# Six of sixteen injection products on GpSimd in one quarter of each Mamba step, and a regrouped opening

## The chip, the cores and the metric

The kernel runs on one core of a Trainium2 chip. The metric is the device time of one execution in microseconds (us). An execution uses five in-order engines: TensorE (PE, matrix products and transposes), VectorE (DVE), ScalarE (ACT), GpSimd (POOL) and SyncE (SP, here the queue from which DMAs are issued). Each engine runs its own list of instructions in order; semaphores are the only ties between them. An instruction that waits for a semaphore holds up all that stands behind it on its engine.

## What is computed

The model adds four sub-layers to a residual of 4096 tokens by 256 features: two Mamba layers (one call), a slot feed-forward network, windowed attention, and the feed-forward network again. The change is in the Mamba part alone, of which this is the core:

```python
def mamba(x, in_w, cw, cb, xp_w, dtp_w, dtp_b, A_log, Dp, out_w):
    ...
    xc = jax.nn.silu(xc)
    dbl = jnp.einsum('ble,re->blr', xc, xp_w)
    dt, Bm, Cm = jnp.split(dbl, [DT_RANK, DT_RANK + D_STATE], axis=-1)
    dt = jax.nn.softplus(jnp.einsum('blr,er->ble', dt, dtp_w) + dtp_b)
    A = -jnp.exp(A_log)
    dA = jnp.exp(dt[..., None] * A)
    dBu = (dt * xc)[..., None] * Bm[:, :, None, :]
    ...
    def step(h, inp):
        dA_t, dBu_t, C_t = inp
        h = dA_t * h + dBu_t
        y = jnp.einsum('ben,bn->be', h, C_t)
        return (h, y)
    ...
    y = ys.transpose(1, 0, 2) + xc * Dp
    y = y * jax.nn.silu(z)
    return jnp.einsum('ble,de->bld', y, out_w)
```

There are 512 inner channels e and 16 states n. `dBu` is what this text calls the injection.

## The kernel before

**Steps, units, quarters.** Each of two layers takes its 4096 tokens in 8 chunks of 512, so Mamba is 16 steps (`ALL`), written `s`. A step has 64 units `k` (`UNITS`): a unit is 4 states by 32 channels on the 128 partitions and 512 tokens along the row. Sixteen units make a quarter (`EG`), and a quarter holds four of the sixteen states for all channels. Four units make a quad. While step s scans, the projections, convolution, softplus and transposes of step p = s + 1 are woven in at fixed units, given by the tables of numbers at the top of the file (`D_...` for VectorE, `A_...` for ScalarE, `G_...` for GpSimd, `P_...` for TensorE).

**A unit.** ScalarE makes the decay, an exponential of 128x512 (`decay`, L541), at most 4 units ahead of the scan (`DEC`). TensorE transposes four 128x128 blocks of products into PSUM (`inject`, L771), at most 2 units ahead. VectorE runs the scan (L415). ScalarE copies the last column of four scanned units at a time (`keep`, L549), eight units after the quad's first in its own list; the copy of quad q stands at unit 4q + 8. GpSimd multiplies the scanned state by C (`output`, L640), in place, and waits at each quad's first unit for that copy (`carry`). TensorE then sums the states (L784).

**The products.** A quarter f = 4s + k//16 is injected from 16 products of 128x512, number j for token block j//4 and state j%4: `u_tok` (dt times x, tokens on partitions) times one column of `B_tok`. They are made one quarter ahead, into two buffers in turn (the names `k_r` and `u_B`). ScalarE makes 13 of them (L563), one at each unit after that unit's decay, and GpSimd three, numbers 3, 7 and 11 (`ON_POOL`), after its outputs of the units 0, 4 and 7 of the quarter (`G_PROD`, L629). At the first unit of a quarter `inject` waits for all sixteen, by two counts, `prod_a` and `prod_p`.

**Around the third quarter.** At unit 42 ScalarE loads the silu table, makes four silus of 128x512 (L512) and one of 128x2048 (L515) and loads the exponential table back; at unit 46 it does the same for softplus (L530, L533). From unit 47 on TensorE transposes the conv output and dt of the next step to tokens, one block after the other (`tok_x` L751, `tok_dt` L760), and VectorE copies the first (L380) and multiplies it by the second (L385) into `u_tok`.

**The opening.** Step s = -1 has no scans: it is the preparation of step 0 alone, and the 16 products of quarter 0 are its last work. On VectorE and TensorE the same blocks alternate one by one over two PSUM banks, each waiting for the one before to be read.

Of the kernel before, what the change touches and what calls it, by code (L numbers as in the profile page):

```python
# [12 lines left out]
P = 128  # L13
# [14 lines left out]
TB = T // P  # L28
# [18 lines left out]
PP = len(ON_POOL)  # L47
PA = NG * TB - PP
FIRST_A = [min(j for j in range(SG * tb, SG * tb + SG) if j not in ON_POOL) for tb in range(TB)]
LAST_V = 3  # L50
EARLY = 3
# [31 lines left out]
G_PROD = (0, 4, 7)  # L83
G_RSTD = 5
# [48 lines left out]
def mamba(nc, x, r, weights, consts, kept_r):  # L133
# [7 lines left out]
    with ExitStack() as ctx:  # L141
# [49 lines left out]
                 "b scan carry hc hc_v ysum prod_a prod_p gated o_mm res").split()  # L191
# [10 lines left out]
        conv_bank = lambda p, ct: PA_ + ct % 2 if p else CT + ct  # L202
        kc = lambda p, base, i, n=1: K[:, p // STEPS, base + i:base + i + n]
# [4 lines left out]
        with nc.Block() as block:  # L208
# [107 lines left out]
            def _(dve):  # L316
# [51 lines left out]
                def tok_B(p):  # L368
                    at(dve, "bt_mm", p + 1)
                    at(dve, "prod_a", PA * NG * (p - 1))  # L370
                    at(dve, "prod_p", PP * NG * (p - 1))
# [3 lines left out]
                def tok_x(p, tb):  # L375
                    at(dve, "xcT_mm", TB * p + tb + 1)
                    if p:
                        at(dve, "prod_a", PA * (NG * p - 1) + AFTER_A[tb])
                        at(dve, "prod_p", PP * (NG * p - 1) + AFTER_P[tb])
                    dve.tensor_copy(uT[:, tb], PS[:, PB_]).then_inc(S["xcT"], 1)  # L380

                def tok_u(p, tb):
                    at(dve, "dtT_mm", TB * p + tb + 1)
                    dve.wait_ge(S["xcT"], TB * p + tb + 1)
                    dve.tensor_tensor(uT[:, tb], PS[:, PA_], uT[:, tb], ALU.mult).then_inc(S["uT"], 1)  # L385
# [42 lines left out]
                for s in steps:  # L428
# [3 lines left out]
                    for k in range(UNITS):  # L432
# [29 lines left out]
                        if k == D_B:  # L462
                            tok_B(p)
                        for n in range(len(D_XT)):
                            if k == D_XT[n]:
                                tok_x(p, n)
                        for n in range(len(D_U)):
                            if k == D_U[n]:
# [3 lines left out]
            def _(act):  # L472
# [49 lines left out]
                def projected(p):  # L522
# [3 lines left out]
                    act.activation(dbl[:], PS[0:XW, PA_], ACT.Copy).then_inc(S["dbl"], 1)  # L526
# [40 lines left out]
                for s in steps:  # L567
                    p = s + 1
                    for k in range(UNITS):
# [5 lines left out]
                        if 0 <= f < ALL * NG and j not in ON_POOL:  # L575
# [4 lines left out]
                        if k == A_HALO and p < ALL:  # L580
                            halo(p)
                        if s < ALL and k == A_SILU:
                            silus(s)
                        if p >= ALL:
# [14 lines left out]
            def _(pool):  # L599
# [42 lines left out]
                for s in steps:  # L642
                    p = s + 1
                    for k in range(UNITS):
# [3 lines left out]
                        for n in range(PP):  # L648
# [1434 lines left out]
```

## Time and profile before

| | us |
|---|---|
| median of 3 executions | 2333.46 |
| lowest and highest | 2328.74, 2335.32 |
| the profiled execution | 2333.48 |
| its span | 2331.7 |
| TensorE, VectorE, ScalarE, GpSimd busy | 2067.5, 1880.3, 1795.9, 1654.9 |

The span is the stretch between the first and the last record. The Mamba part runs until about 1755 us of it. Its steps repeat: VectorE's first scan of a step stands at 62.78 us in step 0, and two equal stretches of 105.35 us that follow hold the same work. Busy shares are means over parts of the program with different limits, so single stretches are read below. "Idle before" in a row is what the engine waited just before it, with what ended the wait.

### The profile page before, as it was taken

What the parts mean: (1) busy time and instruction counts of PE and PEld (TensorE: products, weight loads), DVE (VectorE), ACT (ScalarE), POOL (GpSimd) and SP (SyncE); (2) the same over time, 40 slices, a digit from 0 to 9 for tenths busy, and PEclk for the clock granted to TensorE, in tenths of its full rate; (3) what the DMA queues carried; (4) which work ended last, traced back from release to release, by engine and by line L of the source; (5) the groups of instructions that cost most, each with busy time, mean ns of one, the idle gap of its engine ahead of it and who ended that gap; (6) DMA issues with size and microseconds to landing.
All of it is one profiled execution on the core that took longest, in us unless ns stands there. A gap on an engine that the chain in (4) does not pass through costs nothing. (4 is left out here: it accounts for less than half of the span.)

```text
span 2331.7 us, 40782 instructions
## 1 busy us (share of the span) xinstructions
PE 2067.5 (89%) x14787; PEld 1241.9 (53%) x14787; DVE 1880.3 (81%) x2584; ACT 1795.9 (77%) x3062; POOL 1654.9 (71%) x1448
## 2 busy tenths in 40 slices
PE   5989898998989898989989898989874879999987
PEld 2445455454545455554545454554533557777765
DVE  6788889898988889898988888888988656666655
ACT  3988998989898988989888989989864434455453
POOL 2789889898989889898989898898995253223110
PEclk9999999999999999999999999999996889999998
DMA  7340505142341515142331405041415000000012
GB/s 243 72 114 23 128 13 124 47 100 67 70 108 29 123 54 128 38 117 56 82 96 41 114 23 128 19 118 40 107 55 179 1 10 20 11 15 16 11 40 73
DMA packets 112237, 166.45 MB, mean 71 GB/s; under 512 B 13219, under 2 KB 58531, under 8 KB 111653
## 3 DMA queue, kind: packets, MB, share of 16 engines
q1 hardware_dynamic: 112036, 163.86, 26.8%
q8 instruction: 117, 1.92, 0.4%
q14 instruction: 84, 0.68, 0.1%
HBM read 125.53 MB, written 34.08 MB: 68 GB/s over the span
## 5 line engine op out<-in xcount | busy, mean ns | idle before, releaser
L640 POOL TENSOR_TENSOR h<-h,C_rep 128x512 f32<-128x512 f32 x1021 | 1270.5, 1277 | 196.3 <-ACT h_carry L549 196.3
L415 DVE TENSOR_TENSOR_SCAN h<-decay,h_carry,psum 128x512 f32<-128x512 f32 x768 | 955.7, 1270 | 126.5 <-PE psum L771 93.8
L541 ACT ACTIVATE decay<-dt_rep,A 128x512 f32<-128x512 f32 x1024 | 729.4, 713 | 96.6 <-DVE h L415 93.3
L771 PE MATMUL psum<-ident,u_B 128*128 128x128 f32 x2048 | 322.0, 282 | 125.1 <-DVE h L415 98.2
L771 PEld LDWEIGHTS psum<-ident,u_B 128*128 128x128 f32 x2048 | 235.2, 141 | 310.4 <-DVE h L415 215.2
L771 PEld LDWEIGHTS psum<-ident,k_r 128*128 128x128 f32 x2048 | 243.3, 142 | 248.8 <-issue 124.7
L415 DVE TENSOR_TENSOR_SCAN h<-decay,zero,psum 128x512 f32<-128x512 f32 x256 | 318.8, 1271 | 50.2 <-PE psum L771 34.7
L771 PE MATMUL psum<-ident,k_r 128*128 128x128 f32 x2048 | 309.9, 279 | 14.2 <-DVE h L415 9.0
L563 ACT ACTIVATE u_B<-u_tok,B_tok 128x512 f32<-128x512 f32 x416 | 295.1, 709 | 35.3 <-PE psum L771 35.3
L563 ACT ACTIVATE k_r<-u_tok,B_tok 128x512 f32<-128x512 f32 x416 | 294.4, 710 | 28.9 <-DVE u_tok L385 17.7
L784 PE MATMUL psum<-h,state_sum 128*32 128x512 f32 x2048 | 279.8, 619 | 3.6 <-POOL h L640 3.4
L694 PE MATMUL psum<-x_dt_gated,tap_diag 128*128 128x512 f32 x384 | 189.3, 597 | 0.0
L1773 DVE TENSOR_REDUCE a_row_max<-a_psum 128x4 f32<-128x512 f32 x128 | 87.6, 685 | 82.4 <-PE a_psum L1919 82.4
L1835 ACT ACTIVATE a_probs_T<-a_psum 128x512 f32<-128x512 f32 x128 | 69.6, 595 | 97.8 <-PE a_psum L1929 97.8
L673 PE MATMUL psum<-h_feat,w_x 128*128 128x512 f32 x256 | 135.0, 613 | 1.0 <-ACT h_feat L491 1.0
L673 PE MATMUL psum<-h_feat,w_z 128*128 128x512 f32 x256 | 131.2, 605 | 0.0
L799 PE MATMUL psum<-w_out,x_dt_gated 128*128 128x256 f32 x480 | 122.5, 383 | 0.0
L1839 ACT ACTIVATE a_probs<-a_probs 128x512 f32<-128x512 f32 x128 | 80.4, 629 | 50.1 <-DVE a_probs L1778 50.1
L629 POOL TENSOR_TENSOR k_r<-u_tok,B_tok 128x512 f32<-128x512 f32 x96 | 99.8, 1040 | 19.1 <-DVE u_tok L385 19.1
L629 POOL TENSOR_TENSOR u_B<-u_tok,B_tok 128x512 f32<-128x512 f32 x96 | 100.0, 1042 | 0.0
L1651 POOL TENSOR_TENSOR a_rstd<-a_vareps,a_minushalf 128x4 f32<-128x4 f32 x7 | 7.2, 1023 | 129.9 <-DVE a_vareps L1724 129.9
L799 PEld LDWEIGHTS psum<-w_out,x_dt_gated 128*128 128x128 f32 x480 | 84.2, 190 | 26.6 <-issue 19.7
(238 smaller groups left out, 2877.2 us busy)
## 6 DMA issues: line engine op xcount, KB each, us to landing
dt_rep<-dt_rows SPq DMA_DIRECT2D x256, 256.0 KB, 5.5
C_rep<-C_rows SPq DMA_DIRECT2D x256, 64.0 KB, 2.0
dt_rows<-x_dt_gated SPq DMA_DIRECT2D x32, 512.0 KB, 4.9
residual<-mamba_residual SPq DMA_DIRECT2D x16, 512.0 KB, 4.0
mamba_residual<-residual SPq DMA_DIRECT2D x16, 512.0 KB, 2.9
x_tok<-mamba_residual SPq DMA_DIRECT2D x15, 512.0 KB, 4.4
f_gru_weights<-in_slot_gru_dram SPq DMA_DIRECT2D x2, 2176.0 KB
u_B<-in_x_dram SPq DMA_DIRECT2D x8, 512.0 KB, 9.1
```

Of the source, the lines that this page charges most:

```text
L415: dve.tensor_tensor_scan(h[:, slot(u)], dec[:, u % DEC], PS[:, u % 2], first, ALU.mult, ALU.add)\
L541: act.activation(dec[:, u % DEC], dtr[:, k % EG], ACT.Exp, scale=A[:, s // STEPS, k:k + 1]).then_inc(S["decay"], 1)
L563: act.activation(pr[f % 2][:, tb, :, EW * n:EW * (n + 1)], uT[:, tb].rearrange("p (g e) -> p g e", e=EW), ACT.Copy, scale=BT[:, p % 2, tb, ...
L629: pool.tensor_tensor(pr[f % 2][:, tb, :, EW * n:EW * (n + 1)], uT[:, tb].rearrange("p (g e) -> p g e", e=EW), BT[:, p % 2, tb, SG * ng + n ...
L640: pool.tensor_tensor(h[:, slot(u)], h[:, slot(u)], crep[:, k // EG], ALU.mult).then_inc(S["hc"], 1)
L673: return pe.matmul(PS[:, bank], w[:, kt, ct * P:(ct + 1) * P], hT[:, kt], start=(kt == 0), stop=(kt == KT - 1))
L694: ins = pe.matmul(PS[:, conv_bank(p, ct)], TAPS[:, ct, j - 1], xs[:, ct, DC - 1 - j:DC - 1 - j + T], start=(j == 1), stop=(j == DC - 1))
L771: ins = pe.transpose(PS[:, u % 2, tb * P:(tb + 1) * P], pr[f % 2][:, tb, eg], ident[:])
L784: ins = pe.matmul(PS[EW * q:EW * (q + 1), YB + j % CT], sely[:], h[:, slot(q0 + q)], start=False, stop=(j >= QUADS - CT))
L799: ins = pe.matmul(PS[:, PA_ + i // 2, i % 2 * D:(i % 2 + 1) * D], g[:, ct, i * P:(i + 1) * P], WO[:, ct], start=(ct == 0), stop=(ct == CT ...
L1773: dve.tensor_reduce(mx[:, n % 2], PS[:, n % 2].rearrange("p (h t) -> p h t", h=4), AX, ALU.max)\
L1839: act.activation(pr[:, n % 4], pr[:, n % 4], ACT.Exp, scale=SCALE).then_inc(S["exp"], 1)
```

## The change

Three things are edited.

First, `LATE_POOL`: of the quarter that is formed during a step's third quarter (f % 4 == 3), GpSimd makes six products, numbers 3, 7, 9, 11, 13 and 15, after its outputs of the units 0, 4, 7, 9, 11 and 13 of that quarter (`G_LATE`), and ScalarE ten. The other three quarters keep three and thirteen. The counts that are waited for are now computed by `by_act` and `by_pool`. (`AFTER_P` and `AFTER_A` are written for `LATE_POOL` and a few lines on again for `ON_POOL`; the second holds.)

Second, quarter 0 of step 0: VectorE makes four of its products (`ON_DVE`, `first_product`, counted by `prod_v`), GpSimd three, ScalarE nine.

Third, the rest of the opening (p == 0): each silu waits for its own conv tile instead of for all four, the 12-column copy `halo` comes behind the silus, the x projection writes another PSUM bank, and the transposes of all four token blocks come in one go, conv output first and dt after, into eight different banks. VectorE reads them as four copies and four multiplies.

```diff
+LATE_POOL = (3, 7, 9, 11, 13, 15)
+on_pool = lambda f: LATE_POOL if f % NG == NG - 1 else ON_POOL
...
+def by_pool(f):
+
+    return sum(len(on_pool(e)) for e in range(f))
+
+
+def by_act(f):
+
+    return f * NG * TB - by_pool(f) - (PV if f > 0 else 0)
...
+ON_DVE = (2, 6, 10, 14)
+PV = len(ON_DVE)
...
+G_LATE = (0, 4, 7, 9, 11, 13)
...
+        xp_bank = lambda p: PA_ if p else CT
+        xt_bank = lambda p, tb: PB_ if p else YB + tb
+        dtt_bank = lambda p, tb: PA_ if p else (0, 1, PA_, PB_)[tb]
...
+                def first_product(j):
+
+                    tb, n = j // SG, j % SG
+                    at(dve, "uT", tb + 1)
+                    at(dve, "bt", 1)
+                    dve.tensor_scalar(pr[0][:, tb, :, EW * n:EW * (n + 1)], uT[:, tb].rearrange("p (g e) -> p g e", e=EW),
+                                      BT[:, 0, tb, n:n + 1], None, ALU.mult).then_inc(S["prod_v"], 1)
...
-                        at(act, "conv", CT * (s + 2))
                         for ct in range(CT):
+                            at(act, "conv", CT * (s + 1) + ct + 1)
...
-                        if 0 <= f < ALL * NG and j not in ON_POOL:
+                        if 0 <= f < ALL * NG and j not in on_pool(f) and (f or j not in ON_DVE):
                             product(f, j)
...
-                        for n in range(PP):
-                            if 0 <= f < ALL * NG and k % EG == G_PROD[n]:
-                                product(f, ON_POOL[n])
+                        for j, at_k in zip(on_pool(f), G_LATE if f % NG == NG - 1 else G_PROD):
+                            if 0 <= f < ALL * NG and k % EG == at_k:
+                                product(f, j)
...
                     if eg == 0:
-                        at(pe, "prod_a", PA * (f + 1))
-                        at(pe, "prod_p", PP * (f + 1))
+                        at(pe, "prod_a", by_act(f + 1))
+                        if f == 0:
+                            at(pe, "prod_v", PV)
+                        at(pe, "prod_p", by_pool(f + 1))
```

GpSimd in the third quarter of a step (units 36 to 48; L640 is an output of one unit, L629 a product), before:

```order
L640 TENSOR_TENSOR h<-h,C_rep 128x512 [waits m_carry]
L629 TENSOR_TENSOR u_B<-u_tok,B_tok 128x16x32 [waits m_b,m_bt,m_uT]
L640 TENSOR_TENSOR h<-h,C_rep 128x512 x3
L629 TENSOR_TENSOR u_B<-u_tok,B_tok 128x16x32 [waits m_b,m_bt,m_uT]
L640 TENSOR_TENSOR h<-h,C_rep 128x512 [waits m_carry]
L640 TENSOR_TENSOR h<-h,C_rep 128x512 x3
L640 TENSOR_TENSOR h<-h,C_rep 128x512 [waits m_carry]
L640 TENSOR_TENSOR h<-h,C_rep 128x512 x3
L640 TENSOR_TENSOR h<-h,C_rep 128x512 [waits m_C_loaded3,m_carry]
```

The same place now (L677 is the output, L666 the product):

```order
L677 TENSOR_TENSOR h<-h,C_rep 128x512 [waits m_carry]
L666 TENSOR_TENSOR u_B<-u_tok,B_tok 128x16x32 [waits m_b,m_bt,m_uT]
L677 TENSOR_TENSOR h<-h,C_rep 128x512 x3
L666 TENSOR_TENSOR u_B<-u_tok,B_tok 128x16x32 [waits m_b,m_bt,m_uT]
L677 TENSOR_TENSOR h<-h,C_rep 128x512 [waits m_carry]
L677 TENSOR_TENSOR h<-h,C_rep 128x512
L666 TENSOR_TENSOR u_B<-u_tok,B_tok 128x16x32 [waits m_b,m_bt,m_uT]
L677 TENSOR_TENSOR h<-h,C_rep 128x512 x2
L666 TENSOR_TENSOR u_B<-u_tok,B_tok 128x16x32 [waits m_b,m_bt,m_uT]
L677 TENSOR_TENSOR h<-h,C_rep 128x512 [waits m_carry]
L677 TENSOR_TENSOR h<-h,C_rep 128x512
L666 TENSOR_TENSOR u_B<-u_tok,B_tok 128x16x32 [waits m_b,m_bt,m_uT]
```

The last product moved from behind the output of unit 39 to behind that of unit 45, and two waits for `carry` (units 40 and 44) now stand ahead of it.

VectorE in the opening, from the copy of B to the first scans (L380 and L385 make `u_tok`, L415 is a scan), before:

```order
L372 COPY B_tok<-psum 128x64 [waits m_bt_mm]
L365 TENSOR_SCALAR x_dt_gated<-psum,small 128x512 [waits m_halo,m_dt_mm]
L365 TENSOR_SCALAR x_dt_gated<-psum,small 128x512 [waits m_dt_mm]
L380 COPY u_tok<-psum 128x512 [waits m_xcT_mm]
L385 TENSOR_TENSOR u_tok<-psum,u_tok 128x512 [waits m_xcT,m_dtT_mm]
...
L415 SCALAR_TENSOR_TENSOR h<-decay,zero,psum 128x512 [waits m_b,m_decay] x7
```

And now (L400 and L405 make `u_tok`, L412 is a product, L443 a scan):

```order
L392 COPY B_tok<-psum 128x64 [waits m_bt_mm]
L385 TENSOR_SCALAR x_dt_gated<-psum,small 128x512 [waits m_halo,m_dt_mm]
L385 TENSOR_SCALAR x_dt_gated<-psum,small 128x512 [waits m_dt_mm]
L400 COPY u_tok<-psum 128x512 [waits m_xcT_mm] x4
L405 TENSOR_TENSOR u_tok<-psum,u_tok 128x512 [waits m_xcT,m_dtT_mm] x4
L412 TENSOR_SCALAR k_r<-u_tok,B_tok 128x16x32 [waits m_bt,m_uT] x4
L443 SCALAR_TENSOR_TENSOR h<-decay,zero,psum 128x512 [waits m_b,m_decay] x7
```

Four alternating pairs became four copies, four multiplies and four products.

## Rows read from the trace of the kernel before

**Rows 1.** The page: busy us (share of span), instructions.

```profile
PE 2067.5 (89%) x14787; PEld 1241.9 (53%) x14787; DVE 1880.3 (81%) x2584; ACT 1795.9 (77%) x3062; POOL 1654.9 (71%) x1448
```

**Rows 2.** Windows: us; busy PE, PEld, DVE, ACT, POOL (instructions); clock; DMA; GB/s.

```profile
375.40:480.75 105.35, 96.59 (x542) 53.85 (x540) 92.22 (x94) 94.72 (x161) 92.79 (x81) 1.00 0.32 79
...
356.00:379.00 23.00, 16.79 (x121) 9.99 (x121) 22.59 (x24) 20.22 (x37) 22.88 (x20) 1.00 0.72 162
```

**Rows 3.** Timeline, GpSimd, step 2, units 36 to 48: start, us, instructions, idle before.

```profile
346.17 1.27 POOL L640 TENSOR_TENSOR h<-h,C_rep 128x512 f32<-128x512 f32 x1 [7.07 <-ACT h_carry L549]
347.40 1.03 POOL L629 TENSOR_TENSOR u_B<-u_tok,B_tok 128x512 f32<-128x512 f32 x1
348.40 3.74 POOL L640 TENSOR_TENSOR h<-h,C_rep 128x512 f32<-128x512 f32 x3
352.10 1.04 POOL L629 TENSOR_TENSOR u_B<-u_tok,B_tok 128x512 f32<-128x512 f32 x1
356.12 11.15 POOL L640 TENSOR_TENSOR h<-h,C_rep 128x512 f32<-128x512 f32 x9 [2.98 <-ACT h_carry L549]
```

**Rows 4.** Timeline, TensorE, step 2: transposes of unit 47, then of unit 48.

```profile
353.84 0.60 PE L760 MATMUL psum<-ident,x_dt_gated 128*128 128x128 f32 x4
356.00 0.66 PE L771 MATMUL psum<-ident,u_B 128*128 128x128 f32 x4 [1.55 <-ACT u_B L563]
```

**Rows 5.** Timeline, ScalarE, step 2: decay 47, last product, two carry copies.

```profile
354.61 0.72 ACT L541 ACTIVATE decay<-dt_rep,A 128x512 f32<-128x512 f32 x1
355.24 0.71 ACT L563 ACTIVATE u_B<-u_tok,B_tok 128x512 f32<-128x512 f32 x1
355.85 0.19 ACT L549 ACTIVATE h_carry<-h 128x4 f32<-128x4 f32 x1
...
360.24 0.20 ACT L549 ACTIVATE h_carry<-h 128x4 f32<-128x4 f32 x1
```

**Rows 6.** Timeline, VectorE, step 2: scan 47, copy, scan 48, end of the step.

```profile
355.45 1.27 DVE L415 TENSOR_TENSOR_SCAN h<-decay,h_carry,psum 128x512 f32<-128x512 f32 x1
357.13 0.69 DVE L380 COPY u_tok<-psum 128x512 f32<-128x512 f32 x1 [0.41 <-PE psum L751]
357.74 1.27 DVE L415 TENSOR_TENSOR_SCAN h<-decay,h_carry,psum 128x512 f32<-128x512 f32 x1
...
372.44 5.96 DVE L415 TENSOR_TENSOR_SCAN h<-decay,h_carry,psum 128x512 f32<-128x512 f32 x5
```

**Rows 7.** Windows of the opening, columns as in rows 2: the granted clock.

```profile
60.00:65.00 5.00, 4.24 (x8) 2.15 (x9) 1.28 (x1) 4.97 (x8) 0.00 (x0) 0.50 1.07 241
65.00:70.00 5.00, 4.85 (x23) 3.15 (x21) 3.59 (x3) 5.00 (x10) 0.00 (x0) 0.87 1.10 232
```

**Rows 8.** Timeline, TensorE: first products of Mamba, then the last step.

```profile
60.77 1.12 PE L771 MATMUL psum<-ident,k_r 128*128 128x128 f32 x4 [4.57 <-ACT k_r L563]
...
1721.10 1.93 PE L784 MATMUL psum<-h,state_sum 128*32 128x512 f32 x8 [1.35 <-POOL h L640]
1722.96 1.97 PE L771 MATMUL psum<-ident,u_B 128*128 128x128 f32 x8
```

**Rows 9.** Timeline, GpSimd, last step: product 11, then outputs 40 to 60.

```profile
1721.00 1.05 POOL L629 TENSOR_TENSOR u_B<-u_tok,B_tok 128x512 f32<-128x512 f32 x1
1721.99 25.83 POOL L640 TENSOR_TENSOR h<-h,C_rep 128x512 f32<-128x512 f32 x21
```

**Rows 10.** Timeline of the opening: last conv, projection, its copy, products, first decay.

```profile
37.62 0.75 DVE L358 SCALAR_TENSOR_TENSOR conv_out<-x_dt_gated,small,psum 128x512 f32<-128x512 f32 x1 [1.21 <-PE psum L694]
...
40.79 3.62 PE L724 MATMUL psum<-conv_out,w_xproj 128*64 128x512 f32 x8 [3.21 <-ACT conv_out L512]
...
44.45 0.59 ACT L526 ACTIVATE dt_B_C<-psum 64x512 f32<-64x512 f32 x1 [1.97 <-PE psum L724]
...
52.63 8.08 ACT L563 ACTIVATE k_r<-u_tok,B_tok 128x512 f32<-128x512 f32 x13 [2.27 <-DVE u_tok L385]
...
62.02 0.72 ACT L541 ACTIVATE decay<-dt_rep,A 128x512 f32<-128x512 f32 x1
```

More of the change, by code:

```diff
@@ L46 @@
 ON_POOL = (3, 7, 11)
-PP = len(ON_POOL)
-PA = NG * TB - PP
-FIRST_A = [min(j for j in range(SG * tb, SG * tb + SG) if j not in ON_POOL) for tb in range(TB)]
+LATE_POOL = (3, 7, 9, 11, 13, 15)
+on_pool = lambda f: LATE_POOL if f % NG == NG - 1 else ON_POOL
+FIRST_A = [min(j for j in range(SG * tb, SG * tb + SG) if j not in LATE_POOL) for tb in range(TB)]
+AFTER_P = [sum(j < SG * (tb + 1) for j in LATE_POOL) for tb in range(TB)]
+AFTER_A = [SG * (tb + 1) - n for tb, n in enumerate(AFTER_P)]
+def by_pool(f):
+    return sum(len(on_pool(e)) for e in range(f))
+def by_act(f):
+    return f * NG * TB - by_pool(f) - (PV if f > 0 else 0)
 LAST_V = 3
+ON_DVE = (2, 6, 10, 14)
+PV = len(ON_DVE)
 EARLY = 3
@@ L463, in _ @@
                             tok_B(p)
+                        if p == 0 and k == D_XT[0]:
+                            for n in range(TB):
+                                tok_x(p, n)
+                            for n in range(TB):
+                                tok_u(p, n)
+                            for j in ON_DVE:
+                                first_product(j)
                         for n in range(len(D_XT)):
-                            if k == D_XT[n]:
+                            if p and k == D_XT[n]:
                                 tok_x(p, n)
                         for n in range(len(D_U)):
-                            if k == D_U[n]:
+                            if p and k == D_U[n]:
                                 tok_u(p, n)
@@ L745, in tok_x @@
                 def tok_x(p, tb):
-                    if tb == 0:
+                    if p == 0:
+                        at(pe, "silu", CT)
+                        at(pe, "conv", CT)
+                        at(pe, "x_ev", CT)
+                    elif tb == 0:
                         at(pe, "dt", 3 * (p + 1))
@@ L870, in _ @@
                                 raw_dt(p, n)
+                        if p == 0 and k == P_XT[0]:
+                            for n in range(TB):
+                                tok_x(p, n)
+                            for n in range(TB):
+                                tok_dt(p, n)
                         for n in range(len(P_XT)):
-                            if k == P_XT[n]:
+                            if p and k == P_XT[n]:
                                 tok_x(p, n)
                         for n in range(len(P_DTT)):
-                            if k == P_DTT[n]:
+                            if p and k == P_DTT[n]:
                                 tok_dt(p, n)
```

28 lines of the change are left out of this document (15 added, 13 removed).

## The prediction

> **What bounds the kernel now.** The page comes first [rows 1]: TensorE is busy 89% of the span, VectorE 81, ScalarE 77, GpSimd 71. A reader might stop there: GpSimd has most to spare, so three more products on it look free. But the share is a mean, and the question is which wait ends last where the products are used. So the windows of one step come next [rows 2]. A step takes 105.35 us, of which TensorE is idle 105.35 - 96.59 = 8.8 us, ScalarE 10.6, GpSimd 12.6, VectorE 13.1. In the fourth quarter (the 23 us from 356.00) VectorE is busy 22.59 us, so it sets the pace there and there is nothing to catch up with; in the other three TensorE has 8.8 - (23.00 - 16.79) = 2.6 us idle in all.
>
> The third view is GpSimd's own timeline around units 36 to 48 [rows 3]. It idles 7.07 us and then 2.98 us, and both idles end with `h_carry`: the copy that ScalarE makes of the scanned quad. GpSimd is therefore not idle at a place of its choosing. Its outputs trail the scan: output 40 starts at 356.12, when VectorE has scanned unit 47 and is about to scan 48 [rows 6]. The products stand in the same in-order list, between these outputs.
>
> The fourth view is TensorE's [rows 4]. The transposes of unit 48, the first of a quarter, start at 356.00. They are the first that wait for all sixteen products, and ScalarE's product 15 (355.24, 0.71 us [rows 5]) ends that wait today. GpSimd's last product was done at 353.14 [rows 3].
>
> **The six products of the third quarter.** Product 9 takes the list place that product 11 had (352.10, behind output 39). Products 11, 13 and 15 now stand behind the outputs 41, 43 and 45. So before TensorE may inject unit 48, GpSimd must have gone through six outputs and three products after its wait for the carry of quad 10.
>
> - The start. ScalarE's copy for output 40 stood at 355.85 [rows 5]. Of the three products taken from ScalarE, number 9 (unit 41) stands ahead of the silu block, which by its list waits for VectorE's last conv, so I give it nothing. Numbers 13 and 15 stand between that block and the copy, 0.61 us each (355.24 to 355.85): the copy comes at 354.63. GpSimd started 0.27 us after it (356.12 against 355.85): 354.90.
> - The work. Nine outputs took 11.15 us, 1.24 each; a product holds the list 1.00 us (347.40 to 348.40) [rows 3]. 6 x 1.24 + 3 x 1.00 = 10.4 us, so product 15 ends at 365.3.
> - The second carry, ahead of output 44, was there at 360.24 at the latest [rows 5]; GpSimd reaches that output at 354.9 + 4 x 1.24 + 2 = 361.9. It adds nothing.
>
> TensorE injects unit 48 at 365.4 instead of 356.00: **9.4 us later**. Queued behind that wait on TensorE are the conv transposes of token block 1 and all later injections; on VectorE the copy of block 1 (357.13 [rows 6]), which stands ahead of scan 48 (357.74); on ScalarE the decay of unit 52, which waits for scan 48. ScalarE's relief of three times 0.61 us is spent in that wait. VectorE has nothing else to do meanwhile, and from scan 48 to the step's end its rows touch one another [rows 6], so the delay stays.
>
> What hides it? Nothing that I find: the 2.6 us of TensorE's idle in the other quarters and 0.4 us of VectorE's in the fourth are the most that could be given back, 3.0 us in all. Most of it is single waits of 0.3 to 1 us for the engine next door, which shift along, so I take no give-back and keep 3.0 for the range.
>
> **The clock.** TensorE ends its transposes of unit 47 at 354.4 [rows 4] and then waits 11 us. In the opening a wait of 4.57 us was followed by transposes at 1.12 us instead of 0.66 for four [rows 4, 8], and the granted clock of that window is 0.50, the 1.2 GHz level, rising to 0.87 in the next 5 us [rows 7]. So each stall ends at the lower level. On the path stand four transposes of unit 48 and four of block 1, 0.45 us more each: **0.9 us**. After that VectorE is behind its input again. The Trainium skill (TensorE: Matmul & The Clock Gate, What's actually happening) puts it that the slow state is the default and activity releases it; the trace agrees (0.50 after the wait). Without it the sum would lose 15 x 0.9 = 13.5 us.
>
> Fifteen steps prepare a next one: 15 x (9.4 + 0.9) = 154.5 us. The last step has no softplus. GpSimd ended its third product at about 1722.0 and goes on with outputs back to back [rows 9]; six of them and three products end at 1721.99 + 10.4 = 1732.4, against the injection at 1722.96, which ran at the lower clock already (1.97 us for eight) [rows 8]: 9.5 us. Sum **+164.0 us**.
>
> **The opening.** Before, the silus waited for the last conv (37.62 + 0.75), and TensorE projected from 40.79 in eight matmuls of 0.43 us [rows 10]. Now the first three tiles' silus are done early; six matmuls follow TensorE's last conv at 37.6 and take until 40.2, the last pair until 41.1. The copy behind them moves from 44.45 to 41.1: 3.35 us. Behind it, ScalarE's first product moves from 52.63 to about 49.5 (the four copies no longer wait for dt, but three of them go ahead of the first multiply), and ScalarE makes nine instead of thirteen: 9 x 0.62 = 5.6 against 8.08 us, so it ends at 55.1 instead of 60.71: 5.6 us earlier. VectorE's four products begin after the last multiply, near 51.3. No row has this operation; a copy of this size takes 0.69 us and a scan 1.27 [rows 6], so they end between 54.1 and 56.4: hidden at the near end, 1.3 us late at the far one. I take the copy, which is as simple. The rows of dt that the first decays read are sent only 3.35 us earlier, and the DMA share is above 1 there [rows 7], so the gain lies between 3.3 and 5.6 us. I take **5**.
>
> The table that is written twice (`AFTER_A`) makes VectorE's copy of block 3, at unit 54, wait for three products that ScalarE issues by unit 50; the scan of unit 54 needs decay 54, later in the same list. Nothing.
>
> **Sum.** The profiled execution took 2333.48 us, the median 2333.46. 2333.5 + 164.0 - 5 = 2492.5 us; I say 2492.
>
> **The rivals.**
>
> - *The clock stays low for the whole fourth quarter.* After the wait TensorE has little but 128x128 transposes. At the lower level: 16 x 0.9 for the units' transposes (eight took 1.97 [rows 8]), 4 sums of 1.86 (1721.10 to 1722.96), six sets of transposes for tokens at 0.9: 27.2 us against 22.6 of VectorE's, 4.6 more a step in place of 0.9. 2333.5 + 15 x 14.0 + 9.5 - 5 = 2548. For it: the clock was low in the last step's thin work [rows 8]. Against it: 0.87 five us after the wait [rows 7]. 8%.
> - *Half-absorbed.* The 3.0 us of idle are given back in each step: 2333.5 + 15 x 7.3 + 9.5 - 5 = 2447.5. For it: GpSimd trails the scan less after the stall. Against it: TensorE waited for GpSimd hardly anywhere within a step. 8%.
> - *Faster.* GpSimd's chain isn't last, and what is left is ScalarE's relief between silus and carry copy, 2 x 0.61 us a step, with the opening: 2333.5 - 18 - 5 = 2310. It decides at 354.6, when ScalarE's last product would end: GpSimd would have to be done with product 15 by then, and it hasn't begun output 40. 3%.
>
> **How the numbers follow.** The forecast has 81%. Its own bounds: without the clock term and with the full opening 2478; one us given back per step 16 lower; a clock term twice as long 14 higher. The range 2465 to 2525 leaves out most of the rivals and little else. About 0.3% (7 us) is what a measurement of this kernel can tell from no change. Slower by more than that: 97%; faster: 2%; within: 1%.
>
> **What would show it.** In the changed kernel GpSimd's list should have, in each third quarter, one idle of about 7 us, none of note before output 44, and a new one of some 5 us before output 48, whose carry waits for scan 51. TensorE's first injection of a fourth quarter should wait about 11 us with GpSimd's product (L666) as releaser, at a granted clock below 1 in the slice. The step should measure about 115.6 us. The first scan should start near 57.8 instead of 62.8. The forecast is wrong if unit 48 is injected before GpSimd's sixth product, if the step's period is under 112 us, or if the fourth quarter takes much over 23 us after its first injection.

## The result and the profile after

| | before | after |
|---|---|---|
| median of 4 executions | 2334.24 us | 2492.57 us |
| lowest and highest | 2328.74, 2335.32 | 2490.52, 2492.9 |
| the profiled execution | 2333.48 | 2492.44 |
| its span | 2331.7 | 2490.7 |

The ratio of the times is 1.0684 (95% interval 1.0668 to 1.0701). The changed kernel is 6.8% slower, and the forecast of 2492 us stands within 1 us of the median.

The page first, beside [rows 1]: busy us (share of the span) and instructions.

```profile
PE 2092.7 (84%) x14787; PEld 1267.8 (51%) x14787; DVE 1878.9 (75%) x2588; ACT 1770.7 (71%) x3010; POOL 1701.1 (68%) x1496
```

VectorE and ScalarE were busy for the same time or less, GpSimd was busy for 46 us more and TensorE for 25; the span grew by 159. So most of the added time is waiting, and the page doesn't say where. GpSimd's timeline in the third quarter of step 2 does (L677 is an output, L666 a product); it answers to [rows 3].

```profile
362.57 1.27 POOL L677 TENSOR_TENSOR h<-h,C_rep 128x512 f32<-128x512 f32 x1 [7.06 <-ACT h_carry L584]
363.80 1.04 POOL L666 TENSOR_TENSOR u_B<-u_tok,B_tok 128x512 f32<-128x512 f32 x1
364.80 3.73 POOL L677 TENSOR_TENSOR h<-h,C_rep 128x512 f32<-128x512 f32 x3
368.49 1.03 POOL L666 TENSOR_TENSOR u_B<-u_tok,B_tok 128x512 f32<-128x512 f32 x1
371.30 2.50 POOL L677 TENSOR_TENSOR h<-h,C_rep 128x512 f32<-128x512 f32 x2 [1.77 <-ACT h_carry L584]
373.75 1.03 POOL L666 TENSOR_TENSOR u_B<-u_tok,B_tok 128x512 f32<-128x512 f32 x1
374.75 2.48 POOL L677 TENSOR_TENSOR h<-h,C_rep 128x512 f32<-128x512 f32 x2
377.20 1.03 POOL L666 TENSOR_TENSOR u_B<-u_tok,B_tok 128x512 f32<-128x512 f32 x1
378.19 2.48 POOL L677 TENSOR_TENSOR h<-h,C_rep 128x512 f32<-128x512 f32 x2
380.63 1.03 POOL L666 TENSOR_TENSOR u_B<-u_tok,B_tok 128x512 f32<-128x512 f32 x1
381.63 2.49 POOL L677 TENSOR_TENSOR h<-h,C_rep 128x512 f32<-128x512 f32 x2
391.27 1.26 POOL L677 TENSOR_TENSOR h<-h,C_rep 128x512 f32<-128x512 f32 x1 [7.15 <-ACT h_carry L584]
```

GpSimd waits 7.06 us for unit 36 as before. From output 40 (371.30) to the end of the last product (380.63 + 1.03 = 381.66) it does six outputs and three products without a pause, 10.36 us. After two more outputs it finds the quad of unit 48 not yet scanned and idles 7.15 us.

TensorE's timeline over the same time, beside [rows 4]. L814 transposes products for a unit, L801 and L792 transpose for the tokens.

```profile
370.15 0.60 PE L801 MATMUL psum<-ident,x_dt_gated 128*128 128x128 f32 x4
381.76 1.09 PE L814 MATMUL psum<-ident,u_B 128*128 128x128 f32 x4 [11.02 <-issue]
382.64 1.06 PE L792 MATMUL psum<-ident,conv_out 128*128 128x128 f32 x4
...
385.68 0.66 PE L814 MATMUL psum<-ident,u_B 128*128 128x128 f32 x4 [0.27 <-DVE h L443]
```

The 11.02 us stand as "issue", which says that the profile found no releaser. The times point to it: the transposes start at 381.76, 0.10 us after the end of GpSimd's last product, and experiments 4 and 5 show that they move with it. VectorE's timeline, beside [rows 6] (L443 is a scan, L400 the copy of block 1), and ScalarE's copy for output 40, beside [rows 5]:

```profile
371.75 1.27 DVE L443 TENSOR_TENSOR_SCAN h<-decay,h_carry,psum 128x512 f32<-128x512 f32 x1
383.74 0.69 DVE L400 COPY u_tok<-psum 128x512 f32<-128x512 f32 x1 [10.72 <-PE psum L792]
384.35 1.27 DVE L443 TENSOR_TENSOR_SCAN h<-decay,h_carry,psum 128x512 f32<-128x512 f32 x1
...
371.03 0.19 ACT L584 ACTIVATE h_carry<-h 128x4 f32<-128x4 f32 x1
```

Last, windows of the wait, of the 4 us behind it and of the rest of the quarter. Columns as in [rows 2]: us; busy PE, PEld, DVE, ACT, POOL; clock; DMA; GB/s.

```profile
370.80:381.70 10.90, 0.00 (x0) 0.00 (x0) 2.12 (x3) 4.92 (x10) 10.40 (x10) 0.71 0.74 208
381.50:385.50 4.00, 3.65 (x16) 3.28 (x16) 1.76 (x2) 0.00 (x0) 2.62 (x3) 0.50 0.05 16
385.50:405.00 19.50, 14.23 (x104) 8.24 (x104) 19.50 (x21) 15.50 (x27) 13.73 (x12) 1.00 0.56 130
```

**Where the 159 us are.** The same instruction is followed through both traces:

| | before | after | later by |
|---|---|---|---|
| first scan of step 0 | 62.78 | 59.79 | -2.99 |
| scan of unit 47, step 0 | 142.30 | 140.81 | -1.49 |
| injection of unit 48, step 0 | 142.85 | 150.82 | 7.97 |
| the same, step 14 | 1626.22 | 1773.71 | 147.49 |
| the same, step 15 | 1722.96 | 1880.50 | 157.54 |
| last residual add of Mamba | 1754.73 | 1914.03 | 159.30 |

A step has a period of 105.35 us before and 115.47 after, 10.12 more; some steps are 1.5 us longer in both (experiment 10). What follows Mamba takes as long as it did (577.0 and 576.7 us).

### The profile page after: what moved, and what is told of

Same layout as the page of the kernel before. It is cut to its first block and busy times, and to the rows that moved or that the text cites. A ratio compares the mean times of both kernels' runs of the same rounds, so it can differ in the third digit from the quotient of the medians.

```text
span 2490.7 us, 40838 instructions
## 1 busy us (share of the span) xinstructions
PE 2092.7 (84%) x14787; PEld 1267.8 (51%) x14787; DVE 1878.9 (75%) x2588; ACT 1770.7 (71%) x3010; POOL 1701.1 (68%) x1496
## 5 line engine op out<-in xcount | busy, mean ns | idle before, releaser
L677 POOL TENSOR_TENSOR h<-h,C_rep 128x512 f32<-128x512 f32 x1021 | 1272.5, 1277 | 302.8 <-ACT h_carry L584 302.8
L443 DVE TENSOR_TENSOR_SCAN h<-decay,h_carry,psum 128x512 f32<-128x512 f32 x768 | 954.6, 1269 | 137.8 <-PE psum L814 105.9
L814 PE MATMUL psum<-ident,u_B 128*128 128x128 f32 x2048 | 339.4, 293 | 259.3 <-issue 174.5
L814 PEld LDWEIGHTS psum<-ident,u_B 128*128 128x128 f32 x2048 | 248.3, 148 | 447.0 <-issue 241.8
L814 PEld LDWEIGHTS psum<-ident,k_r 128*128 128x128 f32 x2048 | 243.7, 142 | 251.2 <-issue 124.6
L443 DVE TENSOR_TENSOR_SCAN h<-decay,zero,psum 128x512 f32<-128x512 f32 x256 | 318.6, 1270 | 46.9 <-PE psum L814 33.8
L814 PE MATMUL psum<-ident,k_r 128*128 128x128 f32 x2048 | 310.9, 280 | 16.5 <-DVE h L443 10.0
L598 ACT ACTIVATE u_B<-u_tok,B_tok 128x512 f32<-128x512 f32 x368 | 261.2, 710 | 34.8 <-PE psum L814 34.8
L400 DVE COPY u_tok<-psum 128x512 f32<-128x512 f32 x64 | 43.2, 679 | 173.6 <-PE psum L792 173.6
L666 POOL TENSOR_TENSOR u_B<-u_tok,B_tok 128x512 f32<-128x512 f32 x144 | 149.5, 1038 | 0.0
L666 POOL TENSOR_TENSOR k_r<-u_tok,B_tok 128x512 f32<-128x512 f32 x96 | 100.2, 1044 | 15.5 <-DVE u_tok L405 15.5
```

What stands on the lines that cost most here:

```text
L443: dve.tensor_tensor_scan(h[:, slot(u)], dec[:, u % DEC], PS[:, u % 2], first, ALU.mult, ALU.add)\
L598: act.activation(pr[f % 2][:, tb, :, EW * n:EW * (n + 1)], uT[:, tb].rearrange("p (g e) -> p g e", e=EW), ACT.Copy, scale=BT[:, p % 2, tb, ...
L666: pool.tensor_tensor(pr[f % 2][:, tb, :, EW * n:EW * (n + 1)], uT[:, tb].rearrange("p (g e) -> p g e", e=EW), BT[:, p % 2, tb, SG * ng + n ...
L677: pool.tensor_tensor(h[:, slot(u)], h[:, slot(u)], crep[:, k // EG], ALU.mult).then_inc(S["hc"], 1)
L814: ins = pe.transpose(PS[:, u % 2, tb * P:(tb + 1) * P], pr[f % 2][:, tb, eg], ident[:])
```

## The experiments

In every one of them "unit 48" is the first unit of a step's fourth quarter, and step 2 is shown. A carry is the column that ScalarE copies out of four scanned units. A ratio is to the kernel before.

### 1. The opening alone

```diff
-LATE_POOL = (3, 7, 9, 11, 13, 15)
+LATE_POOL = (3, 7, 11)
-G_LATE = (0, 4, 7, 9, 11, 13)
+G_LATE = (0, 4, 7)
```

> The changed kernel with three products on GpSimd in every quarter, so that only the regrouped opening is left. The trace of the changed kernel has the first scan at 59.79 us against 62.78 before, so the theory that the opening gives what its first scan shows expects about 2331 us (3 less than before). The prediction's term of 5 us expects 2329. A rival, that the head start is lost again in step 0, where the transfers of dt rows set the pace, expects 2334.

Measured: 2329.12 us over 11 runs against 2333.57 over 15, ratio 0.9983 (0.9974 to 0.9991). The first scan stands at 60.00, 2.8 us earlier than before, unit 48 of step 0 at 141.64 against 142.85, only 1.2 us earlier. The opening alone gains 4.5 us at the median, and the rest of the change must cost all of the difference. But the 4.5 us are not simply those of the first scan. From one unit 48 to the next, the trace shows one period of 107.80 and four of 106.83 among the fourteen before, and here three of 106.83 and none of 107.80; all others are about 105.35. What these long periods are is in experiment 10.

### 2. The six late products alone

In the kernel before, the lists `LATE_POOL` and `G_LATE` with their counts, and the opening as it was:

```diff
-                        if 0 <= f < ALL * NG and j not in ON_POOL:
+                        if 0 <= f < ALL * NG and j not in on_pool(f):
                             product(f, j)
...
-                        for n in range(PP):
-                            if 0 <= f < ALL * NG and k % EG == G_PROD[n]:
-                                product(f, ON_POOL[n])
+                        for j, at_k in zip(on_pool(f), G_LATE if f % NG == NG - 1 else G_PROD):
+                            if 0 <= f < ALL * NG and k % EG == at_k:
+                                product(f, j)
```

> The kernel before with the six late products alone and its own opening. If the loss is all in the third quarters, 15 steps of 10.1 us (the step went from 105.35 to 115.47 us) and 9.4 us in the last step make 161 us: 2495 us. If the two parts of the change disturb each other, it differs from 2492.6 by more than the few us of the opening, for example under 2480.

Measured: 2492.05 us, ratio 1.0682 (1.0662 to 1.0702), period 115.47. These products alone make the whole loss. Between this kernel and the changed one no gain of the opening can be told: four runs of each, here from 2488.21 to 2496.54. Nor does one trace tell it closely: with the same opening as the kernel before, this one has its first scan at 67.67 instead of 62.78.

### 3. The same six products at other places

The same six products on GpSimd, but five of them behind the outputs of the quarter's units 0 to 4, and all ahead of the wait for the carry of units 40 to 43:

```diff
-G_LATE = (0, 4, 7, 9, 11, 13)
+G_LATE = (0, 1, 2, 3, 4, 7)
```

> The changed kernel with the same six products on GpSimd, but behind the outputs of the units 0, 1, 2, 3, 4 and 7 of the quarter in place of 0, 4, 7, 9, 11 and 13. The theory is that the place in GpSimd's list costs the time, not the 3 us of work: the last product is again behind output 39, the three more fall into the 7 us in which GpSimd waits for the carry of quad 9, and the first injection of the fourth quarter is again released by ScalarE. It expects 2313 to 2331 us (ScalarE's relief of up to 1.2 us a step either counts or not). The rival, that three more products on GpSimd cost their own length or more wherever they stand, expects 15 x 3 us more than before: 2375 us or above.

Measured: 2311.46 us, ratio 0.9912 (0.9896 to 0.9929), just under the expected 2313. The loss is gone, and the kernel is 22 us faster than before. GpSimd's timeline:

```profile
339.75 1.27 POOL L677 TENSOR_TENSOR h<-h,C_rep 128x512 f32<-128x512 f32 x1 [4.08 <-ACT h_carry L584]
340.98 1.04 POOL L666 TENSOR_TENSOR u_B<-u_tok,B_tok 128x512 f32<-128x512 f32 x1
...
345.67 1.04 POOL L666 TENSOR_TENSOR u_B<-u_tok,B_tok 128x512 f32<-128x512 f32 x1
348.47 11.13 POOL L677 TENSOR_TENSOR h<-h,C_rep 128x512 f32<-128x512 f32 x9 [1.76 <-ACT h_carry L584]
```

These are the outputs of units 36 to 48. The wait for unit 36 is 4.08 us and not 7.06: four products stand ahead of it, where in the changed kernel it is one, and the three more fill 3 us in which GpSimd had nothing to do. The last is done at 346.71. TensorE's and VectorE's timelines:

```profile
347.76 0.60 PE L814 MATMUL psum<-ident,u_B 128*128 128x128 f32 x4
...
347.53 0.69 DVE L400 COPY u_tok<-psum 128x512 f32<-128x512 f32 x1 [0.76 <-PE psum L792]
...
348.93 1.27 DVE L443 TENSOR_TENSOR_SCAN h<-decay,h_carry,psum 128x512 f32<-128x512 f32 x1
350.12 0.67 DVE L400 COPY u_tok<-psum 128x512 f32<-128x512 f32 x1
350.70 1.27 DVE L443 TENSOR_TENSOR_SCAN h<-decay,h_carry,psum 128x512 f32<-128x512 f32 x1
```

Unit 48 is injected without a wait, 1.17 us ahead of scan 47 where before it came 0.55 us behind it. Copy and scan 48 follow scan 47 with no gap (1.77 us from scan to scan; before 2.29 [rows 6]). So GpSimd's load was never the trouble, only where in its list the products stood. The period is 104.65, 0.70 less than before: 14 of these make 10 us. The long periods don't occur here either, the longest is 104.81. Against experiment 1, which has three of 1.47 us more, that makes another 4.4. The dips of the clock that go with the long periods (experiment 10) are not gone: three periods have one, but 4 to 8 us behind the injection of unit 48 and not 20 to 28, and there each costs 0.1 to 0.2 us. This is the one of step 1, columns as above:

```profile
246.40:250.40 4.00, 3.32 (x18) 2.49 (x20) 4.00 (x5) 4.00 (x8) 4.00 (x4) 0.59 0.84 302
```

Why they stand elsewhere was not tried.

### 4 and 5. One late product, walked down the list

Four products on GpSimd, the last (number 15) behind output 41 in experiment 4 and behind output 43 in experiment 5:

```diff
-LATE_POOL = (3, 7, 9, 11, 13, 15)
+LATE_POOL = (3, 7, 11, 15)
-G_LATE = (0, 4, 7, 9, 11, 13)
+G_LATE = (0, 4, 7, 9)
```

In experiment 5 the last line is `G_LATE = (0, 4, 7, 11)`.

> The changed kernel with four late products (3, 7, 11, 15) behind the outputs 32, 36, 39 and 41. The chain behind the carry copy is two outputs and one product, 2 x 1.24 + 1.0 = 3.5 us. ScalarE keeps product 13 and loses 15, so the copy comes 0.6 us earlier: product 15 is done at about 355.24 + 0.27 + 3.5 = 359.0 in the time of step 2 before, against the injection at 356.00. The theory of the chain expects 3.0 us a step and little or no clock term (TensorE waits 4.6 us in all, so up to 0.9 us): 15 x 3.0 to 3.9 + 3 - 2 = 2380 to 2394 us. A rival in which any product behind a carry wait costs the whole 10 us expects 2480; one in which the wait is absorbed expects 2334.

> As the one before with the last product behind output 43 in place of 41: two more outputs, 2.5 us more in the chain, so 5.5 us a step and the clock term of up to 0.9: 15 x 5.5 to 6.4 + 5.5 - 2 = 2420 to 2434 us. The difference to the run with output 41 should be 15 x 2.5 = 37 us or, where the clock term comes in only here, up to 51. A rival in which the number of late products counts and not their place expects no difference.

Measured: 2383.04 us, ratio 1.0214 (1.0195 to 1.0233), and 2427.5 us, ratio 1.04 (1.0373 to 1.0426). GpSimd and TensorE of experiment 4, then of 5:

```profile
358.11 2.49 POOL L677 TENSOR_TENSOR h<-h,C_rep 128x512 f32<-128x512 f32 x2 [2.36 <-ACT h_carry L584]
360.57 1.03 POOL L666 TENSOR_TENSOR u_B<-u_tok,B_tok 128x512 f32<-128x512 f32 x1
...
361.70 1.08 PE L814 MATMUL psum<-ident,u_B 128*128 128x128 f32 x4 [4.66 <-ACT k_r L598]
```

```profile
362.84 4.95 POOL L677 TENSOR_TENSOR h<-h,C_rep 128x512 f32<-128x512 f32 x4 [2.37 <-ACT h_carry L584]
367.75 1.04 POOL L666 TENSOR_TENSOR u_B<-u_tok,B_tok 128x512 f32<-128x512 f32 x1
...
368.89 1.08 PE L814 MATMUL psum<-ident,u_B 128*128 128x128 f32 x4 [7.11 <-issue]
```

In both TensorE starts 0.10 us after the end of that one product (361.60 and 368.79). The profile names ScalarE in one and nothing in the other; the wait moves with GpSimd's product in both. A single product of 1.03 us in the wrong place makes the kernel of experiment 4 50 us slower than the kernel before (2333.3 us in the same series), and 69 us slower than the same four products at early places (experiment 9). The periods are 109.20, 111.66 and, with the change, 115.47. The first difference, 2.46, is two outputs (4.95 - 2.49 us). The second is two outputs and two products (4.48) less 0.61, since the change also takes product 13 from ScalarE and so gets its carry that much sooner; that is 3.87 against the 3.81 measured. Between the two medians lie 44.5 us: 15 x 2.46 make 36.9, and the traces show 4.7 more in three long periods that experiment 4 doesn't have and 2.4 in the last step. So the cost follows the length of the list between carry and product, term by term as the sum has it.

### 6. TensorE kept busy during the wait

The changed kernel with work added that computes nothing: 90 transposes of the identity (128x128) on TensorE, ahead of its wait at unit 48.

```diff
+                    if k == 3 * EG and s + 1 < ALL:
+                        at(pe, "xcT", TB * (s + 1) + 1)
+                        for _ in range(90):
+                            pe.transpose(PS[:, PB_, 0:P], ident[:], ident[:])
```

> The changed kernel with 90 transposes of the identity on TensorE, into a bank that is free, between the transposes of unit 47 and the first injection of the fourth quarter, in 15 steps. They take 90 x 0.108 = 9.7 us at the higher clock and so fit into the wait of 11 us. If the clock term of the prediction is right, the granted clock stays at the 2.4 GHz level, scan 48 comes 0.85 us sooner after the injection (1.74 instead of 2.59 us), and the time is 15 x 0.85 = 13 us less: 2480 us. If the clock has no part in it, 2492; if the transposes themselves run at the lower clock, 19 us each time, 2610 or more.

Measured: 2474.19 us (2472.46 to 2475.37), ratio 1.0607 (1.0591 to 1.0624), 18 us less than the changed kernel and 6 below the expected 2480. TensorE's timeline, GpSimd's last product, VectorE's scan 48, and the window of the transposes:

```profile
369.32 10.04 PE L810 MATMUL psum<-ident 128*128 128x128 f32 x90 [0.35 <-DVE u_tok L400]
380.10 0.63 PE L818 MATMUL psum<-ident,u_B 128*128 128x128 f32 x4 [0.73 <-issue]
...
378.94 1.06 POOL L666 TENSOR_TENSOR u_B<-u_tok,B_tok 128x512 f32<-128x512 f32 x1
...
381.81 1.27 DVE L443 TENSOR_TENSOR_SCAN h<-decay,h_carry,psum 128x512 f32<-128x512 f32 x1
...
370.00:380.00 10.00, 9.37 (x86) 9.13 (x84) 1.25 (x2) 3.96 (x8) 10.00 (x10) 1.00 0.71 190
```

The wait for GpSimd is still there (its last product ends at 380.00, the injection starts at 380.10). But the clock is 1.00, the four transposes take 0.63 us instead of 1.09, and scan 48 follows the injection by 1.71 us instead of 2.59. The period is 114.69, 0.78 less. So 15 steps give 11.7 us. By the end of Mamba the lead is 13.6 us (1900.46 against 1914.03), as much as 15 terms of 0.9 were to give, but in part by luck: 1.3 us of it stand already at scan 47 of step 0 (139.52 against 140.81), ahead of the first added transpose, and the long periods, which occur here too, add up to 0.5 us less. The rest of the gain lies behind Mamba: 573.1 us against 576.7. It is not shown to be the transposes' work, since the kernel of experiment 7, which has none, took 573.1 us there as well. The Trainium skill (TensorE: Matmul & The Clock Gate, Part 4: PE-mode transpose) says that the full clock does not engage for transpose-mode work. Here the measurement decides otherwise: TensorE did nothing but fp32 transposes in that window, at a granted clock of 1.00. (The trace lists them as MATMUL and doesn't say in which mode they ran.)

### 7. The opening without VectorE's products

In the changed kernel ScalarE makes the four opening products back again:

```diff
-ON_DVE = (2, 6, 10, 14)
+ON_DVE = ()
...
-                        if f == 0:
-                            at(pe, "prod_v", PV)
```

> The changed kernel without VectorE's four products in the opening: ScalarE makes 13 again. Read from the trace alone. In the changed kernel the first decay waits 1.12 us for a transfer of dt rows after ScalarE's products and table load. If the transfer is what sets the first scan, moving four products (2.5 us) back costs only what goes beyond that wait: first scan at about 61.2 us instead of 59.79. If ScalarE's products set it, 62.3.

The first scan is at 61.35, and one execution took 2489.77 us; that number tells nothing of 1.6 us. ScalarE's timeline of this kernel:

```profile
51.21 8.07 ACT L598 ACTIVATE k_r<-u_tok,B_tok 128x512 f32<-128x512 f32 x13 [2.67 <-DVE u_tok L405]
59.30 1.28 ACT L576 ACT_TABLE_LOAD   x1
60.59 0.72 ACT L576 ACTIVATE decay<-dt_rep,A 128x512 f32<-128x512 f32 x1
```

and ScalarE's and VectorE's of the changed kernel:

```profile
42.40 0.59 ACT L561 ACTIVATE dt_B_C<-psum 64x512 f32<-64x512 f32 x1 [1.96 <-PE psum L761]
...
50.99 5.62 ACT L598 ACTIVATE k_r<-u_tok,B_tok 128x512 f32<-128x512 f32 x9 [2.67 <-DVE u_tok L405]
...
59.04 0.72 ACT L576 ACTIVATE decay<-dt_rep,A 128x512 f32<-128x512 f32 x1 [1.12 <-DMA dt_rep<-dt_rows]
...
52.67 2.66 DVE L412 TENSOR_SCALAR k_r<-u_tok,B_tok 128x512 f32<-128x512 f32 x4
```

With nine products ScalarE is through with them at 56.61 and could decay at 57.9; the rows of dt arrive 1.12 us later. With thirteen, nothing waits for that transfer. So VectorE's four products are worth 1.6 us at the first scan (61.35 against 59.79; 1.3 counted from the last conv, which starts 0.2 us later here), not the 2.45 of four ScalarE products, because the transfer takes over as the last to arrive. And they are worth nothing ten microseconds on. VectorE's next work that needs memory, in the changed kernel and then in this one:

```profile
71.81 1.08 DVE L366 BATCH_NORM_STATS2 ln_stats<-x_tok 128x6 f32<-128x256 f32 x3 [1.85 <-DMA x_tok<-mamba_residual]
```

```profile
71.23 1.08 DVE L366 BATCH_NORM_STATS2 ln_stats<-x_tok 128x6 f32<-128x256 f32 x3 [0.25 <-DMA x_tok<-mamba_residual]
```

Both wait there for the tokens of the next chunk, and the kernel without the four products is through no later; its scan 47 of step 0 stands at 140.37 against 140.81.

### 8 and 9. How much of experiment 3 is which product

Seven products on GpSimd, so that ScalarE has none behind number 10, all at early places; and four, only number 15 in addition:

```diff
-LATE_POOL = (3, 7, 9, 11, 13, 15)
+LATE_POOL = (3, 7, 11, 12, 13, 14, 15)
-FIRST_A = [min(j for j in range(SG * tb, SG * tb + SG) if j not in LATE_POOL) for tb in range(TB)]
+FIRST_A = [SG * tb for tb in range(TB)]
-G_LATE = (0, 4, 7, 9, 11, 13)
+G_LATE = (0, 1, 2, 3, 3, 4, 7)
```

`FIRST_A` names ScalarE's first product of each token block; as it was written it would find none in the last block. In experiment 9 it stays as it was, with `LATE_POOL = (3, 7, 11, 15)` and `G_LATE = (0, 1, 4, 7)`.

> The run with six early places, and one product more taken from ScalarE: numbers 3, 7, 11, 12, 13, 14 and 15, behind the outputs of the units 0, 1, 2, 3, 3, 4 and 7 of the quarter. ScalarE then has no product between its silus and unit 48. In the trace of the six early places VectorE's copy of token block 0 waits for TensorE, whose list has the transposes of units 46 and 47 and a state sum ahead of it, and decay 47 is ready before the scan. The theory is that ScalarE is no longer last there: the step stays at 104.65 us and the time at 2311 us, give or take 3. The rival, that every 0.61 us taken from ScalarE ahead of unit 48 shortens the step, expects 15 x 0.6 us less or more: 2302 us or below.

> The changed kernel with four late products (3, 7, 11, 15) behind the outputs of the units 0, 1, 4 and 7 of the quarter. Of the three products moved in the run with six early places only number 15 is ScalarE's last work ahead of the injection of unit 48. If it alone makes the 0.7 us a step (105.35 to 104.65), this run has the same period and about 2312 us. If each of the three has a share, the period is about 105.1 us and the time 2323.

Measured: 2314.13 us, ratio 0.9921 (0.9899 to 0.9943), period 104.65; and 2313.94 us, ratio 0.992 (0.99 to 0.9941), period 104.74. Taking four products from the end of ScalarE's list gives no more than taking two, and one gives nearly all: 0.61 of the 0.70 us. That fits the rows of experiment 3, in which copy and scan 48 already touch scan 47 and the copy ahead of scan 47 (347.53) waits 0.76 us for TensorE: a relief of ScalarE beyond that is worth nothing. The three kernels cannot be told apart by their times.

### 10. TensorE filled at the end of each step

The long periods of experiment 1 were not foreseen. In the kernel before, one such step ends like this; window with columns as above, then TensorE's timeline (L784 sums states, L771 transposes products):

```profile
482.00:486.00 4.00, 3.48 (x16) 1.37 (x15) 3.84 (x5) 3.16 (x7) 4.00 (x5) 0.59 1.08 214
...
481.48 0.66 PE L771 MATMUL psum<-ident,u_B 128*128 128x128 f32 x4 [0.52 <-DVE h L415]
482.65 1.11 PE L771 MATMUL psum<-ident,u_B 128*128 128x128 f32 x4 [0.52 <-DVE h L415]
483.69 1.93 PE L784 MATMUL psum<-h,state_sum 128*32 128x512 f32 x8
```

The clock falls while TensorE works in short pieces with idles of 0.52 us between them, and eight sums take 1.93 us instead of the 1.06 that eight take at the full clock. In the traces of the kernel before, of experiment 1 and of the changed kernel, each of the twelve long periods has such a dip 20 to 28 us behind the injection of unit 48, and none of the others has one there (107.80 has two dips). To see whether the dips make the long steps, identity transposes, which compute nothing, were added to the kernel before:

```diff
+                        if 0 <= s < ALL - 1 and k >= UNITS - 6:
+                            at(pe, "xcT", TB * (s + 2))
+                            for _ in range(4):
+                                pe.transpose(PS[:, PB_, 0:P], ident[:], ident[:])
```

> The kernel before with four transposes of the identity more on TensorE in each of the last six units of 15 steps, where TensorE idles 0.52 us a unit. In the kernel before five of the first 14 periods are longer than 105.35 us: 107.80 and four of about 106.84, and in the one looked at the granted clock falls to 0.59 at the end of the step (482 to 486 us). If that dip is what lengthens them, the transposes (0.43 us a unit, into the idle) leave all periods at 105.35 to 105.8 us and the time at 2334 - 2.4 - 4 x 1.5 = 2325 us. If the long steps have another cause, the time is 2334 or, where the transposes delay the injections, above.

The same window of this kernel:

```profile
482.00:486.00 4.00, 3.92 (x27) 2.19 (x25) 4.00 (x6) 3.62 (x8) 4.00 (x4) 1.00 1.07 212
```

In this trace the clock is 1.00 through all fourteen periods and no long one is left, so the dips are what lengthens them. But every period is now 105.70, 0.35 us more than the 105.35 of the undisturbed ones: the added transposes stand in front of work. The time is 2331.1 us over 12 runs against 2333.5 over 17, ratio 0.999 (0.9978 to 1.0002), which can't be told from none. The expectation of 2325 was too high in its gain. Only one execution has a trace, one of the fastest (2325.66); the twelve reach up to 2335.53, so it is not shown that the dips stay away in all of them. And of this one's lead of 7.8 us over the profiled execution before, 2.1 stand at the end of Mamba; 5.7 lie behind it, where nothing was added. Why a dip falls into some steps and not into others stays open.

## Why the prediction was right, by its own steps

- **What bounds the kernel.** That GpSimd's outputs trail the scan, and that the products stand in the same list behind a carry, is what experiments 3 to 5 show. GpSimd's busy share of 71% told nothing of it; the kernel with six products takes 22 us less than before or 158 more, by their places alone.
- **The start.** The carry copy was to come 1.22 us earlier by the relief of ScalarE. Relative to scan 47 it stands 0.40 us behind its start before (355.85 and 355.45 [rows 5, 6]) and 0.72 us ahead of it after (371.03 and 371.75): 1.12. GpSimd follows 0.27 us later, as forecast.
- **The work.** Six outputs and three products: 10.36 us against 10.4 forecast. The second carry, ahead of output 44, was there: GpSimd begins that output at 378.19 with no idle.
- **The injection of unit 48.** 0.55 us behind the start of scan 47 before, 10.01 after: 9.46 us later against 9.4.
- **The clock.** Injection to scan 48 went from 1.74 to 2.59 us, 0.85 against 0.9, and experiment 6 takes 0.78 a step back by keeping the clock up. The rival of a clock that stays low through the quarter falls by the third window: 1.00 from 4 us after the wait. The row at 353.84 [rows 4], which the forecast calls the transposes of unit 47, is that of dt for token block 0 (L760); TensorE does end its work there, so the wait it starts is read rightly.
- **What hides it.** Hardly anything: 9.46 + 0.85 = 10.31 at scan 48, 10.12 in the period. About 0.2 us a step are given back, not the 3.0 of the half-absorbed rival. 15 steps at 10.12 instead of 10.3 are 2.7 us less than the sum had.
- **The last step.** The lateness grows from 147.49 to 157.54 between the injections of steps 14 and 15. Less the clock's 0.85 of step 14, which shows only behind its injection, that leaves 9.2 against 9.5. Behind scan 48 of that step another 1.8 us are lost, 1.2 of them at scan 52, for which the forecast had no term; the granted clock there reads 0.50 and 0.58 in the 8 us from 1880, and 0.61 and 1.00 before in those from 1722. TensorE's row at the injection is the counterpart of [rows 8]:

```profile
1880.50 1.94 PE L814 MATMUL psum<-ident,u_B 128*128 128x128 f32 x8 [9.43 <-issue]
```

- **The opening**, the one term that was mis-sized. 5 us were forecast, with the first scan near 57.8; it comes at 59.79, 2.99 us earlier than before and under the forecast's own bound of 3.3. Two reasons show in the rows. The last conv of this execution started 1.2 us later than before's (38.83 against 37.62), so ScalarE's products began at 50.99 and not near 49.5. That is no effect of the change: in the traces of the old opening this conv starts between 37.62 and 39.14, in those of the new one between 37.72 and 39.10. Counted from it, the first scan follows after 20.96 us instead of 25.16, 4.2 us sooner. The copy of the projection is 2.05 us earlier in the trace, 3.3 relative to that conv, as the 3.35 of the forecast. And the rows of dt arrive 1.12 us after ScalarE is ready, the limit behind the forecast's lower bound. What it did not see is the transfer of the next chunk's tokens (1.85 us of waiting at 71.81): by scan 47 of step 0 only 1.49 of the 2.99 us are left (1.2 to 2.8 in the seven experiments with the new opening and four products on VectorE). VectorE's four products are hidden (52.67 to 55.33, 0.47 to 1.26 us each, by the near bound). In the time as a whole the opening alone made 4.5 us, but of these, by its trace, 2.45 are the long first period that it happens not to have, and 1.5 the fourth of the others.
- **The "faster" rival.** It priced the relief of ScalarE at 1.22 us a step. Where the products stand early, the period falls by 0.70, since VectorE's rows then touch. It was to give 2310 and experiment 3 took 2311.46, but partly by luck: what the smaller relief lacks (8 us in 15 steps) the missing long periods make up (8.4 us over the fourteen periods of before).
- **What would show it.** The idle before output 48 is 7.15 us, not some 5, a size for which the forecast had no working. The releaser at TensorE is "issue", not GpSimd's product; the 0.10 us between the two in four kernels, and the walk of experiments 4 and 5, name it. The period is 115.47 against 115.6.
- **Not foreseen:** the long periods of 1.5 us at clock dips. There are four of 106.83 and one of 107.80 before, four of 117.04 after, so they nearly cancel. The total is closer than its parts: the sum was 2.7 us too high by the period, 2.1 by the long periods and too low by 3.5 with the opening (5 forecast, 1.5 left at scan 47) and by 1.8 with the end of the last step. That the sum hits within 1 us is luck; its main term, 9.4 us a step, is not.

## What to carry to other kernels

Before work is moved to the engine with the lowest busy share, look at what its list waits for between the moved instruction's new place and the point where the result is needed; every instruction behind the last of these waits counts at full length. Put the moved work ahead of that wait, where the engine idles anyway: with the same six products the kernel took 2311 us there and 2492 behind it, and one product of 1 us behind it cost 69 against the same product ahead of it. When the moved work is hidden, read which engine's rows follow one another without a gap before moving more.

## What the runs showed of the hardware

TensorE at a granted clock of 1.00 took four 128x128 transposes in 0.60 to 0.66 us and at 0.50 in 1.06 to 1.12. After an 11 us wait in step 2 it was at 0.50 for 4 us and then at 1.00. Ninety transposes of the identity kept it at 1.00 in the same wait. It also fell to 0.59 over 4 us in which TensorE was 3.48 us busy with idles of 0.52 us, and of 0.71 at most in the 10 us before; such a dip lengthened a step by 1.5 us, and with the idles filled the one trace taken has none. The same idles stand in steps without a dip. A VectorE product of 128x512 by one column per partition took 0.67 us in the mean of four (0.47 to 1.26), the same product 0.71 on ScalarE and 1.04 on GpSimd. The part behind Mamba, in which all twelve kernels are the same, took 571.2 to 577.0 us in the twelve traces: a difference of a few us between two traces is not by itself the edit's.
